# Probabilities become the stationary operand of the value product, and the softmax division moves behind it

## The reference

```python
logits = jnp.where(mask, -jnp.inf, logits)
m = jnp.max(logits, axis=-1, keepdims=True)
e = jnp.exp(logits - m)
exp_sink = jnp.exp(s - m)
w = e / (jnp.sum(e, axis=-1, keepdims=True) + exp_sink)
out = jnp.einsum('bhmqk,bkhd->bqhmd', w, v).reshape(Bv, Tv, N_HEADS * HEAD_DIM)
return out @ out_w.T + out_b
```

## Time and profile before

| | |
|---|---|
| three runs | 1277.99 us median (1277.72 to 1279.0) |
| profiled execution, span | 1277.5 us (the page gives no other time for it) |
| TensorE busy | 1098.2 us, 86% |
| VectorE busy | 983.0 us, 77% |
| ScalarE busy | 751.2 us, 59% |
| GpSimd busy | 414.7 us, 32% |
| clock of TensorE over the span | 0.944 of full |

### The profile page before, as it was taken

How to read it: one execution, slowest core, us unless ns; L and a number is a source line. 1 busy time by engine, 2 the same in 40 slices (tenths; PEclk the granted TensorE clock), 3 DMA queues, 4 the chain that set the end, 5 groups by cost and what they waited for, 6 DMA issues and landing times.

```text
span 1277.5 us, 27391 instructions
## 1 busy us (share of the span) xinstructions
PE 1098.2 (86%) x7440; PEld 971.9 (76%) x7441; DVE 983.0 (77%) x3081; ACT 751.2 (59%) x2218; POOL 414.7 (32%) x573
## 2 busy tenths in 40 slices
PE   4699999999999983899999999999996079999993
PEld 1478888878888872799999999999985067777773
DVE  5599998989989998688888888888885444445425
ACT  2266666666666663777787787778775023434321
POOL 4455554555545447001010100100000533336422
PEclk9599999999999995899999999999997589999997
DMA  8100000000000001000000000100001433334212
GB/s 308 69 22 2 23 21 1 21 1 21 21 1 21 1 2 41 2 1 22 1 21 0 21 21 0 70 0 0 1 1 52 163 125 123 123 123 162 81 58 82
DMA packets 26840, 58.40 MB, mean 46 GB/s; under 512 B 3051, under 2 KB 18283, under 8 KB 25579
## 3 DMA queue, kind: packets, MB, share of 16 engines
q1 hardware_dynamic: 18748, 47.50, 10.6%
q10 hardware_dynamic: 6480, 5.90, 1.4%
q0 software_dynamic: 1536, 4.20, 1.0%
HBM read 45.00 MB, written 12.58 MB: 45 GB/s over the span
## 4 chain that ended last, share of the span: by engine, by line
PE 68%; DVE 16%; issue 7%; ACT 5%; DMA 2%; POOL 1%; SPq 1%; DVEq 1%; ACTq 0%; POOLq 0%
PE psO L636 14%; PE psS L608 9%; PE psX L619 9%; PE psP L655 8%; PE psY L690 5%; PE psS L805 4%; PE psX L805 4%; PE psO L819 4%; PE psT L666 3%; DVE pbuf L1176 2%; PE psT L675 2%; DVE pbuf L1192 2%; DVE bufB L1198 1%; ACT pbuf L880 1%; POOL xg L546 1%
## 5 line engine op out<-in xcount | busy, mean ns | idle before, releaser
L880 ACT ACTIVATE pbuf<-pbuf,nmax 128x256 f32<-128x256 f32 (+3 forms) x512 | 266.8, 522 | 171.4 <-DVE nmax L1176 160.0
L636 PE MATMUL psO<-bufB 128*128 128x256 f32 x1632 | 256.7, 293 | 12.0 <-DVE bufB L1202 11.2
L608 PE MATMUL psS<-bufA 128*128 128x256 f32 (+3 forms) x1024 | 216.0, 316 | 19.5 <-DVE bufA L1234 17.2
L636 PEld LDWEIGHTS psO<-bufB 128*128 128x128 f32 x1632 | 212.9, 189 | 23.2 <-issue 12.7
L1198 DVE TENSOR_TENSOR bufB<-psX,bufB 128x512 fp32r<-128x512 f32 x272 | 186.4, 685 | 29.2 <-ACT bufB L853 27.2
L853 ACT ACTIVATE bufB<-psX 128x512 fp32r<-128x512 f32 x272 | 160.4, 590 | 58.8 <-PE psO L636 48.7
L608 PEld LDWEIGHTS psS<-bufA 128*128 128x128 f32 x1024 | 148.7, 193 | 36.9 <-DVE nmax L1176 25.8
L619 PE MATMUL psX<-idn,pbuf 128*128 128x128 f32 x1088 | 166.8, 276 | 2.4 <-DVE bufB L1198 1.9
L655 PE MATMUL psP<-wbufs,hTh 128*128 (+1 forms) x512 | 162.9, 359 | 1.6 <-DVE bufB L1227 1.6
L1192 DVE TENSOR_SCALAR pbuf<-pbuf,rden 128x256 f32<-128x256 f32 (+3 forms) x384 | 153.3, 454 | 4.5
L619 PEld LDWEIGHTS psX<-idn,pbuf 128*128 128x128 f32 x1088 | 124.2, 140 | 17.8 <-issue 8.6
(11 more groups left out here) (187 smaller groups left out, 2304.2 us busy)
## 6 DMA issues: line engine op xcount, KB each, us to landing
mrawV<-in_w_moe SPq DMA_DIRECT2D x8, 1536.0 KB, 6.3
mrawP<-in_w_moe SPq DMA_DIRECT2D x16, 768.0 KB, 4.8
xg<-uN SPq DMA_DIRECT2D x1, 3200.0 KB, 18.3
yg<-uN SPq DMA_DIRECT2D x1, 3200.0 KB, 26.3
wraw<-in_w_attn SPq DMA_DIRECT2D x8, 384.0 KB, 3.1
wraw<-in_w_ffn SPq DMA_DIRECT2D x8, 384.0 KB, 3.0
xin<-xg ACTq DMA_DIRECT2D x23, 128.0 KB, 2.0
yg<-ysb ACTq DMA_DIRECT2D x22, 128.0 KB, 1.7
```

Source lines behind the costliest of these rows:

```text
L608: last = mm(psS[j % 2][:, 0:n], qT[:, s % NT, j * P:(j + 1) * P], kT[:, c, k0:k0 + n], start=(c == 0), stop=(c == 1))
L636: last = mm(psO[:, 0:2 * P], lhsT, pairs(pT)[:, r], start=(k == 0 and n == 0), stop=(k == L.ntiles(s) - 1 and n == 5))
L880: nc.scalar.activation(pj, pj, ACT.Exp, bias=nmax[:, s % 4, j:j + 1], scale=-1.0, accum_out=sums[:, s % 4, j:j + 1]).then_inc(a_exp, 1)
```

## The change

The turned probabilities of one head and key tile become the stationary operand and the values move: `vcat` holds the high part of a tile's values in 64 columns and the low part in the next 64. For each head one matmul with the high part of the probabilities moves all 128 columns, and one with their low part moves the first 64. The result has the queries on the partitions, in psO a block of 128 columns for each head: 64 with the result, 64 with the cross product of the low values. ScalarE copies the cross part (`out_cross`), VectorE adds the two (`out_sum`), GpSimd multiplies by the inverse sum (`normalise`, now on 128 x 256 results instead of the probabilities), and TensorE turns the result by two transposes into psY (`turn_out`). `out_hi` and `out_lo` then read psY instead of psO, and `out_project` writes to the same bank. The multiplications of the probabilities on VectorE and ScalarE are gone. `out_project` goes to the end of TensorE's step (in the causal layer before the last `values`), and `add_y` to the start of VectorE's next one.

```diff
     def turn_probs(g, s, k):
         if k == 0:
-            wait(pe, v_norm, L.unit(g, s))
-            wait(pe, a_norm, L.unit(g, s))
+            wait(pe, a_exp, L.head(g, s, QM - 1))
...
     def values(g, s, k):
         slot = L.kt_slot(s, k)
         if k == 0:
-            wait(pe, v_ol, L.unit(g, s - 1))
+            wait(pe, v_os, L.unit(g, s - 1))
             wait(pe, v_vl, L.unit(g, s))
         wait(pe, v_pl, L.kt(g, s, k))
         kv = L.first_tile(s) + k
-        pairs = lambda p: p[:, slot, :].rearrange("p (i r q) -> p r i q", r=2, q=P)
-        n = 0
-        for v, pT in ((0, pTh), (1, pTh), (0, pTl)):
-            for r in range(2):
-
-                lhsT = vpad[:, v, kv, HD:3 * HD] if r == 0 else vpad[:, v, kv, 0:2 * HD]
-                last = mm(psO[:, 0:2 * P], lhsT, pairs(pT)[:, r],
-                          start=(k == 0 and n == 0), stop=(k == L.ntiles(s) - 1 and n == 5))
-                n += 1
+        end = k == L.ntiles(s) - 1
+        for j in range(QM):
+            q = slice(j * P, (j + 1) * P)
+            mm(psO[:, j * 2 * HD:(j + 1) * 2 * HD], pTh[:, slot, q], vcat[:, kv, :],
+               start=(k == 0 and j == 0), stop=False, skip_group_check=True)
+            last = mm(psO[:, j * 2 * HD:j * 2 * HD + HD], pTl[:, slot, q], vcat[:, kv, 0:HD],
+                      start=False, stop=(end and j == QM - 1), skip_group_check=True)
         last.then_inc(s_PV, 1)
+
+    def turn_out(g, s):
+        wait(pe, g_on, L.unit(g, s))
+        wait(pe, v_y, L.unit(g, s - 1))
+        o = osum[:, s % 2, :, :].rearrange("p h d -> p (h d)")
+        for i in range(2):
+            last = nc.tensor.transpose(psY[:, i * P:(i + 1) * P], o[:, i * P:(i + 1) * P], idn[:, :])
+        last.then_inc(s_ot, 1)
```

On GpSimd:

```diff
+    def normalise(g, s, L=L):
+        wait(pool, v_os, L.unit(g, s))
+        wait(pool, v_rden, L.unit(g, s))
+        o = osum[:, s % 2, :, :]
+        nc.gpsimd.tensor_tensor(o, o, rden[:, s % 4, :].unsqueeze(2).broadcast_to([P, QM, HD]), ALU.mult)\
+          .then_inc(g_on, 1)
...
+        if exists(g, s - 3):
+            normalise(g, s - 3)
         if s in (0, 1, 2) and exists(g, NT):
             split_piece(g + 1, s)
```

On ScalarE:

```diff
-    def normalise(g, s):
-        wait(act, v_rden, L.unit(g, s))
-        for j in range(L.by_vector, QM):
-            pj = probs[:, s % 4, j, 0:L.ntiles(s) * P]
-            last = nc.scalar.activation(pj, pj, ACT.Copy, scale=rden[:, s % 4, j:j + 1])
-        last.then_inc(a_norm, 1)
...
+    def out_cross(g, s):
+        wait(act, s_PV, L.kt_all(g, s))
+        wait(act, v_os, L.unit(g, s - 2))
+        copy(ocross[:, s % 2, :, :], psO[:, :].rearrange("p (h c d) -> p h c d", c=2, d=HD)[:, :, 1, :])\
+            .then_inc(a_oc, 1)
...
     def out_hi(g, s):
-        wait(act, s_PV, L.kt_all(g, s))
+        wait(act, s_ot, L.unit(g, s))
         wait(act, s_Y, L.unit(g, s - 2))
-        copy(oh[:, s % 2, :], psO[:, 0:2 * P]).then_inc(a_oh, 1)
+        copy(oh[:, s % 2, :], psY[:, 0:2 * P]).then_inc(a_oh, 1)
```

On VectorE:

```diff
         V.reciprocal(rden[:, s % 4, :], d[:, s % 4, :]).then_inc(v_rden, 1)
-        wait(dve, v_rden, L.unit(g, s))
-        n = L.ntiles(s) * P
-        for j in range(L.by_vector):
-            pj = probs[:, s % 4, j, 0:n]
-            last = V.tensor_scalar(pj, pj, rden[:, s % 4, j:j + 1], None, ALU.mult)
-        last.then_inc(v_norm, 1)
...
+    def out_sum(g, s):
+        wait(dve, a_oc, L.unit(g, s))
+        wait(dve, s_ot, L.unit(g, s - 2))
+        V.tensor_tensor(osum[:, s % 2, :, :], psO[:, :].rearrange("p (h c d) -> p h c d", c=2, d=HD)[:, :, 0, :],
+                        ocross[:, s % 2, :, :], ALU.add).then_inc(v_os, 1)
```

More of the change, by code:

```diff
@@ L105, in rounds @@
             step(g, s)
-    for s in range(NT + 5):
+    for s in range(NT + 6):
         step(NKV - 1, s)
@@ L189, in build @@
         o = 0
-        vpad = bufB[:, 0:2 * NT * 3 * HD].rearrange("p (c t n) -> p c t n", c=2, t=NT)
-        o = 2 * NT * 3 * HD
+        vcat = bufB[:, 0:NT * 2 * HD].rearrange("p (t n) -> p t n", t=NT)
+        o = NT * 2 * HD
         pTh = bufB[:, o:o + 2 * QM * P].rearrange("p (c n) -> p c n", c=2)
@@ L198, in build @@
         ol = bufB[:, o:o + 2 * 2 * P].rearrange("p (c n) -> p c n", c=2)
+        ocross = sb_att("ocross", [P, 2, QM, HD])
+        osum = sb_att("osum", [P, 2, QM, HD])
         pbuf = sb_att("pbuf", [P, 4 * QM * SEQ])
@@ L321, in build @@
         v_rden = sem("v_rden")
-        v_norm = sem("v_norm")
-        a_norm = sem("a_norm")
+        a_oc = sem("a_oc")
+        v_os = sem("v_os")
+        g_on = sem("g_on")
+        s_ot = sem("s_ot")
         s_X = sem("s_X")
@@ L709, in step_window @@
                     if exists(g, s - 4):
-                        out_project(g, s - 4)
+                        turn_out(g, s - 4)
                     if now:
@@ L719, in step_window @@
                         turn_k(g, s + 1)
+                    if exists(g, s - 4):
+                        out_project(g, s - 4)
                 def step_causal(g, s):
@@ L916, in project_hi @@
                     wait(act, s_PV, L.kt_all(g - 1, s % NT // TB * TB + TB - 1 + s // NT * NT))
-                    copy(vpad[:, 0, s % NT, HD:2 * HD], psP[:, HQ + HD:QKV]).then_inc(a_vh, 1)
+                    copy(vcat[:, s % NT, 0:HD], psP[:, HQ + HD:QKV]).then_inc(a_vh, 1)
                 def write_qT(g, s):
@@ L936, in step_window @@
                     if exists(g, s - 3):
-                        out_hi(g, s - 3)
+                        out_cross(g, s - 3)
                     if nk > 1:
@@ L941, in step_window @@
                         exp_head(g, s, 1)
-                    if back:
-                        normalise(g, s - 1)
+                    if exists(g, s - 4):
+                        out_hi(g, s - 4)
                     if exists(g, s + 1):
@@ L1186, in normalise @@
                         d = den
+                    wait(dve, g_on, L.unit(g, s - 4))
                     V.reciprocal(rden[:, s % 4, :], d[:, s % 4, :]).then_inc(v_rden, 1)
-                    wait(dve, v_rden, L.unit(g, s))
-                    n = L.ntiles(s) * P
-                    for j in range(L.by_vector):
-                        pj = probs[:, s % 4, j, 0:n]
-                        last = V.tensor_scalar(pj, pj, rden[:, s % 4, j:j + 1], None, ALU.mult)
-                    last.then_inc(v_norm, 1)
                 def probs_lo(g, s, k):
@@ L1247, in step_window @@
                     nk = L.ntiles(s - 2) if exists(g, s - 2) else 0
+                    if exists(g, s - 5):
+                        add_y(g, s - 5)
                     if back:
@@ L1257, in step_window @@
                     if exists(g, s - 3):
-                        out_lo(g, s - 3)
+                        out_sum(g, s - 3)
                     if now:
@@ L1264, in step_window @@
                     if exists(g, s - 4):
-                        add_y(g, s - 4)
+                        out_lo(g, s - 4)
                     if ahead:
@@ L1284, in step_causal @@
                     if exists(g, s - 3):
-                        out_lo(g, s - 3)
+                        out_sum(g, s - 3)
                     if nk > 1:
                         probs_lo(g, s - 2, 1)
-                    if exists(g, s - 4):
-                        add_y(g, s - 4)
                     if now:
                         mask_max(g, s, 2)
+                    if exists(g, s - 4):
+                        out_lo(g, s - 4)
                     if exists(g, s + 1):
```

15 lines of the change are left out of this document (5 added, 10 removed).

## The result

| | before | after |
|---|---|---|
| median of four runs | 1278.5 us | 1418.4 us (1414.0 to 1422.1) |
| ratio | | 1.109, 95% interval [1.107, 1.111] |
| span of the profiled run | 1277.5 us | 1420.1 us |
| predicted | | 1361 us, range 1322 to 1398 |

The account below looks back on a forecast made before the run. TensorE was taken as the bound, so work added to its queue is paid nearly in full. The terms 52 + 28 - 24 + 10 + 14 + 0 + 4 = 84 us on 1277.5 gave 1361.5 us, range 1322 to 1398.

Parts of the forecast that it names:

- The value product: TensorE's `values`: 8 matmuls at 0.112 us instead of 6 at 0.117 for each of 272 key tiles, +52 us.
- The turned result: TensorE's `turn_out`: two more transposes for each of 128 units, 256 at 0.11 us, +28 us.
- Windowed layer, removed: TensorE's waits for VectorE's `out_lo` in the windowed layer go, with shorter unlisted waits: -24 us, ends 15 and 40.
- added in each step: Windowed layer: `out_project` waits about 0.2 us for the same step's `out_lo` in 48 steps, +10 us.
- Windowed layer, added once in rounds 1 to 6: Weight piece 2 holds GpSimd's queue, so its division is late and TensorE waits 2.5 us a round: +14 us.
- Causal layer: Waits for `write_kT` go (18 us), `out_project` comes 0.55 us late in two of four steps (18 us): net 0.
- At the end of each layer: The last unit has one hop more (copy, sum, division, turn, about 2 us): +4 us.
- B: Rival: all VectorE's waits on TensorE vanish and nothing new comes, +26 us, 1304 and up to 1335; chance 0.13.
- C: Rival: the chain from `turn_out` to `out_project` is 0.5 us later in 128 steps, +64 more, about 1425; chance 0.11.
- D: Rival: faster than before, the value product runs by its columns, not its loads, 1211 by columns alone; chance 0.06.

Follow-up runs that it names:

- e7_short_piece: The changed kernel with two waits left out of VectorE's loop bodies and GpSimd's third weight piece moved from step 2 to step 4: 1359.7 us.
- e9_after_place: The changed kernel with 45 real instructions (two waits in each) added at the start of VectorE's program: 1388.8 us.
- e1_pad: The changed kernel with 60 empty instructions at the start of VectorE's program, none of which has a row in the trace: 1418.1 us.
- e10_before_place: The kernel before the change with 45 real instructions added at the start of VectorE's program: 1267.9 us.
- e2_piece: The changed kernel with GpSimd's third weight piece prepared in step 4 of a round instead of step 2: 1399.4 us.
- e11_before_swap: The kernel before the change with 232 real instructions added at the start of VectorE's program: 1302.7 us.
- e5_short: The changed kernel with two waits left out of VectorE's loop bodies (on g_on in normalise, on s_ot in out_sum): 1386.7 us.

## Why the prediction was wrong, step by step

The direction was right. Two steps of the sum failed: the wait for GpSimd was charged with its length (14 us) and cost 28, and VectorE's jump back at the end of its causal loop stood at nothing and cost 30.

The spans of four profiled runs split the 142.6 us between before and after. Before to `e7_short_piece` (1357.8 us) is 80.3, where the sum without GpSimd's term had 84 - 14 = 70. From there to `e9_after_place` (1385.7) it is 27.9, GpSimd's queue, where the sum had 14. From there to after (1420.1) it is 34.4, where the sum had nothing. Of this, 30.1 is in the causal layer: the place of VectorE's code. The rest is a net 4 us at and behind the end of the windowed layer, where the half clock began earlier (524.7 us) than in `e9_after_place` (543.2); in `e1_pad`, with the same instructions as after, it began at 539.4, so this rest is not charged to the jump.

- **"The value product": right.** 0.112 us a matmul was forecast and 0.112 measured between loads, also for the 64-column ones that had no row.
- **"The turned result": right.** In layers without disturbance the two terms are the whole difference. A key tile costs 0.19 more and a unit 0.22, so 112 key tiles and 64 units make 35 us in the windowed layer, 160 and 64 make 44 in the causal one. Measured, `e7_short_piece` against `e10_before_place`, from `add_y` to `add_y`: 427.3 - 391.3 = 36.0, and 470.5 - 427.7 = 42.8.
- **"Windowed layer, removed", 24, and "added in each step", 10:** the net gain of 14 us did not come. Against the kernel before the windowed layer of `e7_short_piece` is 28.3 us longer, which looks like a gain of 7; but against `e10_before_place`, where both loops jump fast as well, it is 36.0 longer, the two terms above and nothing off. The 7 us are the kernel before's own slow jump: moving its code took 8 us out of this layer (399.0 to 391.3), with the operations of the waits for `out_lo` untouched. These waits were 10.0 us over 19 times, and with the code moved 5.3 over 14:

```profile
PE psT L675 <- ACT bufA L853: 12.0, 15, 1.0
PE psO L636 <- DVE bufB L1204: 5.3, 14, 2.4
```

- **"Windowed layer, added once in rounds 1 to 6", 14: the step that failed on its price.** Place, number (six) and length were right: forecast 2.5 us, listed up to 2.2 with 0.2 more to the next possible start. But the sum charged a wait with its length. Removing the six gave 19 us by medians (`e2_piece`) and 27.9 by spans (`e9_after_place` to `e7_short_piece`), that is 5 to 14 us more than their length. In `e9_after_place` half clock follows five of the six, for 3 to 10 us each.
- **"Causal layer", net 0: right** for its own waits (61.5 us rounds; four steps 30.8 in place of 27.9), and **incomplete: the step that failed on a term it lacked.** The prediction costed VectorE's instructions and never its jump, though the trace of before had a slow one: at the windowed loop's turn VectorE idles for 2.5 us with nothing to wait for (line below), the jump takes 2.8 us, and with the code moved the rounds are 1.6 us shorter (53.3 to 51.7). The change moved the causal body by 12 instructions to the front and made it one longer, and so it touched a third block. That is 30 of the 57 us by which the forecast missed. The kernel before at the windowed turn:

```profile
159.80 0.16 DVE L1184 TENSOR_TENSOR den<-sums,esink 128x4 f32<-128x4 f32 x1 [2.54 <-issue]
```

- **"At the end of each layer", 4:** 10 measured (59.2 us between the layers before, 68.4 in `e7_short_piece`, and 1 at the end). Most of it is again GpSimd's order. Behind the windowed layer GpSimd adds the attention's result to `xN`, sixteen operations that TensorE's next layer waits for. Before, they start 12 us ahead of the last `add_y` and end 2.0 us behind it (486.3 against 484.25). Now they stand behind the last division, and end 8.2 us behind it (520.0 against 511.75). Before, then `e7_short_piece`:

```profile
472.03 0.73 POOL L523 TENSOR_TENSOR yN<-yN,modb 128x256 f32<-128x256 f32 x1
```

```profile
507.50 0.61 POOL L491 TENSOR_TENSOR osum<-osum,rden 128x256 f32<-128x256 f32 x1 [3.41 <-DVE osum L1212]
508.07 0.73 POOL L533 TENSOR_TENSOR yN<-yN,modb 128x256 f32<-128x256 f32 x1
519.27 0.72 POOL L534 TENSOR_TENSOR xN<-xN,yN 128x256 f32<-128x256 f32 x1
```

  TensorE's idle time between the layers grows by the same 6.2 us, from 19.3 to 25.5. The sum had no term for this; no experiment removed it. The other 3 us lie between TensorE's restart and the first `add_y` of the causal layer, where the new hops are; they were not taken apart.
- **The rivals.** B fails, waits did not vanish. C forecast 1425, nearest to the measured time, and was wrong on the cause: `out_project` waits 34 times, 20.9 us in all, not 64 us. D's column rate is refuted by the pace of the loads, 0.11 us. The 81 ns of the Trainium skill (TensorE: Matmul & The Clock Gate, Back-to-back issue gap) do not agree with that pace either. Slower had the chance 0.94 and came. VectorE's share came out at 71% of the windowed and 67% of the causal stretch, where under 70% was forecast for both.

With both disturbances cured the kernel took 1359.7 us, against 1347 from the terms without GpSimd's. That it lies next to the forecast of 1361.5 is chance: the forecast had reckoned with one of the two. On equal footing (the loops of both kernels in two blocks, the weight piece moved in the one) the change costs 1359.7 - 1267.9 = 92 us.

## What to carry to other kernels

Count the instructions of every loop body that a change lengthens or shifts, on each engine, and look at the gap called "issue" at the loop's turn before and after: in this kernel of some 1400 us, 45 instructions more at the start gave 30 us. The page's row for the instruction queue tells at once whether a loop is fetched again at each turn. Price a wait of a full TensorE by what runs behind it, not by its length alone. When an engine gets one more operation in a step, look at everything that stands behind it in that queue, beyond the loop too. A padding experiment counts only if the trace shows more instructions; and where, as here, the stationary tile changes with each matmul, halving the moving columns from 256 bought next to nothing (0.117 to 0.112 us).

## What was unexpected in the hardware

- VectorE's jump back took 0.27 to 0.37 us when the body lay in two blocks of 256 instructions and 2.7 to 3.5 us when it touched three, in all 18 attention loops of the nine kernels in the table (`e5_short` and `e7_short_piece` counted both), whatever else they held. In the slow case the profile's instruction queue moved about five packets more for each turn. ScalarE's bodies of 234 to 259 records and GpSimd's of up to 134 always took 0.16 to 0.30 us; no run here put one of them over three blocks.
- Waits of 2.2 to 2.7 us in a stream of matmuls were followed by 3 to 10 us at 1.2 GHz in 8 of 11 cases in the kernel after, and in 2 of 5 in `e11_before_swap`; in one run waits of 0.95 us were, twice. So the same kernel has causal rounds of 64.1 and 68.7 us side by side. The slow jump in five causal turns cost the kernel before 15 us (`e11_before_swap`) and the kernel after 30.
- Empty instructions (`nop(nofuse=True)`) left no row in any trace; 232 instructions of two waits each, on a count long reached, took 15 us at the start of VectorE's program.
